# One causal attention and gated FFN layer on one core: one head's row moves on ScalarE's queue, new orders, the last row block in two column halves

## The reference

```
xn  = layernorm(x)                                   # no scale or shift
q   = xn @ w_q.T  (32 heads of 128), k, v = xn @ w_k.T, xn @ w_v.T (8 heads of 128)
p   = softmax(causal(q k^T / sqrt(128)))             # 4 query heads share a k/v head
s   = concat_heads(p @ v) @ w_dense.T
g   = silu(ffn(xn))    # three 512x512 layers of +1/-1 weights, two relu between
out = x + s * g
```

## Time and profile before

| | |
|---|---|
| median of 3 runs | 921.42 us (917.15 to 922.13) |
| the profiled execution | 921.1 us |
| its span, first to last instruction | 919.4 us |
| TensorE matmul busy | 895.9 us, 97% |
| VectorE, ScalarE, POOL busy | 650.1, 517.7, 480.9 us |
| mean granted TensorE clock | 0.996 of full speed |
| DMA queue of SyncE, share of the 16 DMA engines | 64.7% |

### The profile page before, as it was taken

One profiled execution on the slowest core, in us unless ns is written; L12 is line 12 of the kernel. 1 busy time (PEld: TensorE's weight loads), 2 busy tenths in 40 slices (PEclk: granted clock), 3 DMA queues, 4 the chain that ended last, 5 costly groups with the idle time before them and its releaser, 6 DMA issues.

```text
span 919.4 us, 15763 instructions
## 1 busy us (share of the span) xinstructions
PE 895.9 (97%) x4187; PEld 747.9 (81%) x4187; DVE 650.1 (71%) x1145; ACT 517.7 (56%) x1096; POOL 480.9 (52%) x388
## 2 busy tenths in 40 slices
PE   7999999999999999999999999989999999989997
PEld 6888888887878888888888887878878887778886
DVE  7436777777777787688767787767777786577844
ACT  4405665556546665466556654655556663475652
POOL 5302565546554665346654655445554754346674
PEclk9999999999999999999999999999999999999999
DMA  7176857577766866586747666684757675465662
GB/s 251 47 213 189 229 131 176 133 205 166 161 133 184 220 147 151 163 239 134 185 132 196 180 161 133 180 220 113 179 136 201 174 165 137 121 201 126 140 168 92
DMA packets 215561, 152.01 MB, mean 165 GB/s; under 512 B 23664, under 2 KB 180848, under 8 KB 215536
## 3 DMA queue, kind: packets, MB, share of 16 engines
q1 hardware_dynamic: 215536, 151.71, 64.7%
HBM read 67.90 MB, written 27.39 MB: 104 GB/s over the span
## 4 chain that ended last, share of the span: by engine, by line
issue 49%; POOL 31%; PE 15%; DMA 2%; DVE 1%; SPq 1%; POOLq 1%; ACT 0%; DVEq 0%
POOL pt_lo L830 22%; POOL w_lo L855 4%; POOL wd_lo L855 3%; PE ps_m L1341 3%; PE ps_m L1217 2%; PE ps_m L1219 2%; PE ps_m L1218 2%; PE ps_s L1326 2%; POOL v_lo L843 1%; PE ps_o L1217 1%; PE ps_o L1219 1%; PE ps_o L1218 1%; PE ps_s L1219 1%; PE ps_s L1218 1%; PE ps_s L1217 1%
## 5 line engine op out<-in xcount | busy, mean ns | idle before, releaser
L830 POOL TENSOR_TENSOR pt_lo<-pt_lo,pt_hi 128x512 fp32r<-128x512 f32 x248 | 324.1, 1334 | 308.8 <-ACT pt_hi L963 308.7
L1073 DVE CUSTOM_DVE_ANT_0 ps_s<-ps_s,mask 128x32 f32<-128x32 f32 (+31 forms) x256 | 181.5, 715 | 106.1 <-PE ps_s L1219 104.8
L963 ACT ACTIVATE pt_hi<-pt_lo 128x512 fp32r<-128x512 f32 x288 | 169.0, 627 | 102.2 <-PE ps_o L1219 58.4
L917 ACT ACTIVATE prob_odd<-ps_s,small 128x160 f32<-128x160 f32 (+15 forms) x128 | 95.9, 751 | 62.3 <-DVE small L1073 59.6
L1217 PE MATMUL ps_m<-xn_hi,w_hi 128*128 128x512 f32 x320 | 125.4, 392 | 2.2 <-DVE q_lo L1176 2.2
L1218 PE MATMUL ps_s<-k_lo,q_hi 128*128 128x480 f32 (+15 forms) x384 | 127.2, 331 | 0.0
L1219 PE MATMUL ps_s<-k_hi,q_lo 128*128 128x480 f32 (+15 forms) x384 | 126.8, 330 | 0.0
L1217 PE MATMUL ps_o<-pt_hi,v_hi 128*128 128x512 f32 x288 | 118.0, 410 | 8.4 <-POOL pt_lo L830 7.9
L1219 PE MATMUL ps_m<-xn_hi,w_lo 128*128 128x512 f32 x320 | 125.6, 393 | 0.0
L1218 PE MATMUL ps_m<-xn_lo,w_hi 128*128 128x512 f32 x320 | 125.4, 392 | 0.0
L1217 PE MATMUL ps_s<-k_hi,q_hi 128*128 128x480 f32 (+15 forms) x384 | 124.8, 325 | 0.0
(11 more groups left out here) (122 smaller groups left out, 1494.3 us busy)
## 6 DMA issues: line engine op xcount, KB each, us to landing
pt_lo<-prob_odd SPq DMA_DIRECT2D x128, 128.0 KB, 2.9
pt_lo<-prob_even SPq DMA_DIRECT2D x128, 112.0 KB, 2.3
pt_lo<-prob_odd SPq DMA_DIRECT2D x128, 96.0 KB, 2.2
raw<-wqk SPq DMA_DIRECT2D x40, 256.0 KB, 4.6
pt_lo<-prob_even SPq DMA_DIRECT2D x128, 80.0 KB, 2.6
inv_rows<-inv SPq DMA_DIRECT2D x32, 256.0 KB, 4.2
raw<-wd SPq DMA_DIRECT2D x32, 256.0 KB, 3.9
at_lo<-inv SPq DMA_DIRECT2D x32, 256.0 KB, 3.7
```

The lines of the kernel that those rows point to most:

```text
L830: pool.tensor_tensor(pt_lo[:, slot, :], pt_lo[:, slot, :].bitcast(F32), pt_hi[:, hi_slot, :], ALU.subtract).then_inc(land_lo, 1)
L917: act.activation(prob_tile(i, tile), as_tiles(score_row(i, tile)), ACT.Exp, scale=-1.0, bias=neg_max[:, slot:slot + 1], accum_out=row_sum[ ...
L963: act.activation(pt_hi[:, hi_slot, :], pt_lo[:, LAND_AT[i] + j, :].bitcast(F32), ACT.Copy).then_inc(land_hi, 1)
L1073: dve.tensor_tensor_reduce(out=scores, in0=scores, in1=mask[:, S - width(i % BLOCKS, tile):S], scale=-1.0, scalar=BIG, op0=ALU.add, op1=AL ...
```

## The change

Of each move of rows 4 to 7 the DMA of head 3 is issued by ScalarE, as a new token `amove.i.b` in its list; SyncE keeps heads 0 to 2. The lists of the body and of the last group are new on all engines, with the same tokens otherwise. In the last group dense.7 is done as two halves of 256 columns in the two banks, all 24 matmuls at the place of dense.7.3; its gate and its addition of x come before it (x + y * silu), and each half is multiplied by silu in place, added and stored by itself.

The diff; the POOL and VectorE lists of the body and most of the last group's lists are left out.

```diff
@@ -46,6 +46,8 @@
 BANKS4 = 4
 BY_DRAM = 4
 MOVES = TILES * HEADS
+
+ACT_HEADS = {i: (3,) for i in range(BY_DRAM, BLOCKS)}
 
 LANDS = [1 if n < BY_DRAM else MOVES for n in range(BLOCKS)]
 LANDINGS = (sum(LANDS[0::2]), sum(LANDS[1::2]))
...
 BODY = {
     "pe": """
-        unit.q2.1.0 scores.1.0 scores.1.1 scores.1.2 scores.1.3 unit.q2.1.1 unit.q2.1.2
-        unit.q2.1.3 scores.2.0 scores.2.1 unit.k.1.0 scores.2.2 scores.2.3 unit.k.1.1 weigh.0.0
-        scores.3.0 unit.k.1.2 scores.3.1 scores.3.2 unit.k.1.3 unit.q3.1.0 unit.q3.1.1 unit.q3.1.2
-        unit.q3.1.3 scores.3.3 unit.q0.1.0 unit.q0.1.1 unit.q0.1.2 unit.q0.1.3 unit.q1.1.0
-        unit.q1.1.1 unit.q1.1.2 unit.q1.1.3 dense.0.0 weigh.1.0 dense.0.1 weigh.1.1 scores.4.0
-        scores.4.1 dense.0.2 dense.0.3 unit.q1.0.0 scores.4.2 unit.q1.0.1 scores.4.3 unit.q1.0.2
-        scores.5.0 unit.q1.0.3 dense.1.0 dense.1.1 scores.5.1 scores.5.2 dense.1.2 weigh.2.0
-        dense.1.3 unit.q2.0.0 scores.5.3 weigh.2.1 scores.6.0 weigh.2.2 weigh.3.0 weigh.3.1
-        scores.6.1 weigh.3.2 unit.q2.0.1 unit.q2.0.2 weigh.3.3 unit.q2.0.3 dense.2.0 scores.6.2
-        dense.2.1 dense.2.2 dense.2.3 scores.6.3 unit.q0.0.0 unit.q0.0.1 scores.7.0 weigh.4.0
-        weigh.4.1 weigh.4.2 unit.q0.0.2 unit.q0.0.3 weigh.4.3 weigh.4.4 scores.7.1 scores.7.2
-        dense.3.0 weigh.5.0 dense.3.1 weigh.5.1 scores.7.3 dense.3.2 weigh.5.2 weigh.5.3 dense.3.3
-        weigh.5.4 weigh.5.5 unit.k.0.0 unit.k.0.1 unit.k.0.2 unit.k.0.3 unit.q3.0.0 unit.q3.0.1
-        weigh.6.6 unit.q3.0.2 unit.q3.0.3 dense.4.0 dense.4.1 dense.4.2 weigh.6.5 dense.4.3
-        scores.8.0 weigh.6.4 scores.8.1 weigh.6.3 weigh.6.2 scores.8.2 dense.5.0 scores.8.3
-        weigh.6.1 dense.5.1 dense.5.2 weigh.6.0 weigh.7.0 weigh.7.1 dense.5.3 weigh.7.2 weigh.7.3
-        weigh.7.4 weigh.7.5 weigh.7.6 weigh.7.7 dense.6.0 dense.6.1 dense.6.2 dense.6.3 dense.7.0
-        dense.7.1 dense.7.2 dense.7.3
+        scores.1.0 scores.1.1 scores.1.2 unit.q2.1.0 scores.1.3 unit.q2.1.1 scores.2.0 scores.2.1
+        unit.q2.1.2 scores.2.2 unit.q2.1.3 unit.q3.1.0 scores.2.3 unit.q3.1.1 unit.q3.1.2
+        scores.3.0 unit.q3.1.3 unit.q1.1.0 scores.3.1 scores.3.2 weigh.0.0 unit.q1.1.1 unit.q1.1.2
+        unit.q1.1.3 unit.k.1.0 unit.k.1.1 unit.k.1.2 scores.3.3 unit.k.1.3 unit.q0.1.0 unit.q0.1.1
+        unit.q0.1.2 unit.q0.1.3 dense.0.0 dense.0.1 dense.0.2 dense.0.3 scores.4.0 unit.q0.0.0
+        scores.4.1 unit.q0.0.1 scores.4.2 weigh.1.0 weigh.1.1 scores.4.3 unit.q0.0.2 scores.5.0
+        unit.q0.0.3 unit.q2.0.0 unit.q2.0.1 scores.5.1 unit.q2.0.2 scores.5.2 unit.q2.0.3
+        dense.1.0 dense.1.1 dense.1.2 scores.5.3 weigh.2.0 weigh.2.1 weigh.2.2 dense.1.3
+        scores.6.0 scores.6.1 weigh.3.0 weigh.3.1 weigh.3.2 weigh.3.3 dense.2.0 dense.2.1
+        dense.2.2 scores.6.2 scores.6.3 weigh.4.0 dense.2.3 unit.q1.0.0 unit.q1.0.1 weigh.4.1
+        unit.q1.0.2 scores.7.0 weigh.4.2 weigh.4.3 unit.q1.0.3 dense.3.0 scores.7.1 dense.3.1
+        weigh.4.4 scores.7.2 dense.3.2 weigh.5.0 scores.7.3 weigh.5.1 weigh.5.2 dense.3.3
+        weigh.5.3 unit.k.0.0 unit.k.0.1 weigh.5.4 weigh.5.5 unit.k.0.2 unit.k.0.3 unit.q3.0.0
+        unit.q3.0.1 unit.q3.0.2 unit.q3.0.3 dense.4.0 dense.4.1 dense.4.2 scores.8.0 dense.4.3
+        scores.8.1 scores.8.2 weigh.6.6 weigh.6.5 weigh.6.4 dense.5.0 weigh.6.3 weigh.6.2
+        dense.5.1 weigh.6.1 weigh.6.0 weigh.7.0 dense.5.2 weigh.7.1 dense.5.3 weigh.7.2 weigh.7.3
+        scores.8.3 weigh.7.4 weigh.7.5 weigh.7.6 weigh.7.7 dense.6.0 dense.6.1 dense.6.2 dense.6.3
+        dense.7.0 dense.7.1 dense.7.2 dense.7.3
     """,
     "act": """
-        exp.1.0 exp.1.1 exp.1.2 exp.1.3 hi.land.0.0 hi.unit.q2.1 hi.split.wd0 hi.split.wd1 exp.2.0
-        exp.2.1 exp.2.2 hi.split.wd2 exp.2.3 hi.weigh.0 hi.unit.k.1 exp.3.0 hi.split.wd3 exp.3.1
-        hi.unit.q3.1 exp.3.2 exp.3.3 hi.unit.q0.1 hi.land.1.0 hi.land.1.1 hi.split.q0 hi.unit.q1.1
-        hi.split.q1 hi.split.q2 hi.vload.1 hi.weigh.1 exp.4.0 exp.4.1 exp.4.2 exp.4.3 hi.unit.q1.0
-        exp.5.0 hi.land.2.0 hi.land.2.1 hi.land.2.2 exp.5.1 exp.5.2 hi.land.3.0 hi.land.3.1
-        hi.land.3.2 hi.split.q3 exp.5.3 hi.land.3.3 hi.split.k hi.weigh.2 exp.6.0 exp.6.1
-        hi.unit.q2.0 hi.land.4.0 hi.land.4.1 hi.land.4.2 hi.land.4.3 exp.6.2 hi.weigh.3 exp.6.3
-        hi.land.4.4 hi.unit.q0.0 exp.7.0 hi.land.5.0 hi.land.5.1 hi.land.5.2 hi.land.5.3 exp.7.1
-        hi.land.5.4 hi.land.5.5 hi.weigh.4 exp.7.2 exp.7.3 hi.land.6.6 hi.land.6.5 hi.unit.k.0
-        hi.land.6.4 hi.land.6.3 hi.land.6.2 hi.weigh.5 hi.unit.q3.0 hi.land.6.1 hi.land.6.0
-        exp.8.0 exp.8.1 exp.8.2 hi.land.7.0 hi.land.7.1 hi.land.7.2 exp.8.3 hi.land.7.3
-        hi.land.7.4 hi.land.7.5 hi.weigh.6 hi.land.7.6 hi.land.7.7 hi.weigh.7 hi.vload.0
+        exp.1.0 exp.1.1 exp.1.2 exp.1.3 exp.2.0 exp.2.1 hi.unit.q2.1 hi.land.0.0 exp.2.2
+        hi.split.wd0 exp.2.3 hi.unit.q3.1 hi.split.wd1 hi.split.wd2 hi.vload.1 exp.3.0 hi.weigh.0
+        hi.unit.q1.1 exp.3.1 hi.split.wd3 exp.3.2 hi.unit.k.1 exp.3.3 hi.unit.q0.1 hi.split.q0
+        hi.land.1.0 hi.land.1.1 hi.split.q1 exp.4.0 hi.split.q2 exp.4.1 exp.4.2 hi.weigh.1 exp.4.3
+        hi.unit.q0.0 exp.5.0 hi.land.2.0 hi.land.2.1 exp.5.1 hi.land.2.2 hi.unit.q2.0 exp.5.2
+        hi.land.3.0 amove.4.0 hi.land.3.1 hi.land.3.2 exp.5.3 hi.land.3.3 hi.weigh.2 amove.4.1
+        amove.4.2 amove.4.3 exp.6.0 exp.6.1 amove.5.0 hi.land.4.0 hi.land.4.1 hi.land.4.2
+        hi.land.4.3 exp.6.2 hi.weigh.3 exp.6.3 hi.land.4.4 amove.5.1 amove.5.2 amove.5.3
+        hi.split.q3 hi.split.k hi.unit.q1.0 exp.7.0 hi.land.5.0 hi.land.5.1 exp.7.1 hi.land.5.2
+        hi.land.5.3 hi.land.5.4 hi.weigh.4 exp.7.2 hi.land.5.5 exp.7.3 amove.6.0 amove.6.1
+        amove.6.2 amove.6.3 hi.unit.k.0 amove.7.0 amove.7.1 amove.7.2 hi.unit.q3.0 hi.land.6.6
+        hi.land.6.5 hi.land.6.4 hi.weigh.5 hi.land.6.3 amove.7.3 hi.land.6.2 hi.land.6.1
+        hi.land.6.0 exp.8.0 exp.8.1 hi.land.7.0 hi.land.7.1 hi.land.7.2 hi.land.7.3 exp.8.2
+        hi.land.7.4 hi.weigh.6 hi.land.7.5 hi.land.7.6 hi.land.7.7 exp.8.3 hi.weigh.7 hi.vload.0
     """,
...
     "sp": """
-        load.wd0 load.wd1 load.wd2 vload.1 dw.1 load.wd3 load.q0 rw.1 dr.1 load.q1 rr.1 load.q2
-        dw.2 rw.2 dw.3 load.q3 dr.2 rr.2 load.k rw.3 dr.3 move.4.0 move.4.1 move.4.2 move.4.3 rr.3
-        rw.4 move.5.0 move.5.1 move.5.2 move.5.3 rr.4 rw.5 move.6.0 move.6.1 move.6.2 move.6.3
-        rr.5 rw.6 move.7.0 move.7.1 move.7.2 move.7.3 rr.6 rw.7 rr.7 dw.8 vload.0 rw.8 dr.8 rr.8
+        load.wd0 load.wd1 load.wd2 vload.1 dw.1 rw.1 load.wd3 dw.2 load.q0 dr.1 load.q1 rr.1
+        load.q2 dr.2 rw.2 dw.3 load.q3 rw.3 load.k dr.3 rr.2 move.4.0 move.4.1 move.4.2 move.4.3
+        rr.3 rw.4 move.5.0 move.5.1 move.5.2 rr.4 move.5.3 rw.5 move.6.0 move.6.1 move.6.2
+        move.6.3 rr.5 rw.6 move.7.0 move.7.1 move.7.2 move.7.3 rr.6 rw.7 rr.7 vload.0 dw.8 rw.8
+        dr.8 rr.8
     """,
 }
 LAST = {
...
     "act": """
-        exp.1.0 exp.1.1 exp.1.2 exp.1.3 hi.land.0.0 exp.2.0 exp.2.1 hi.unit.q3.1 hi.split.wd0
-        exp.2.2 exp.2.3 hi.unit.q2.1 hi.split.wd1 hi.split.wd2 hi.vload.1 exp.3.0 hi.unit.q1.1
-        exp.3.1 hi.split.wd3 exp.3.2 hi.weigh.0 hi.unit.q0.1 hi.land.1.0 exp.3.3 hi.land.1.1
...
+        exp.1.0 exp.1.1 exp.1.2 exp.1.3 hi.land.0.0 exp.2.0 exp.2.1 hi.unit.q0.1 hi.split.wd0
+        exp.2.2 hi.split.wd1 hi.unit.q3.1 hi.split.wd2 exp.2.3 hi.vload.1 exp.3.0 hi.unit.q2.1
+        hi.weigh.0 hi.split.wd3 hi.unit.k.1 exp.3.1 hi.land.1.0 hi.unit.q1.1 build.0.0 build.0.1
+        build.0.2 build.0.3 exp.3.2 exp.3.3 hi.land.1.1 exp.4.0 build.1.0 build.1.1
...
     "dve": """
...
-        lo.hidden.1.1.3 gate.0 gate.1 lo.land.7.7 gate.2 mul.weigh.7 gate.3 lo.weigh.7 gate.4
-        lo.dense.6 gate.5 gate.6 lo.dense.7 gate.7 add_x.7
...
+        gate.5 lo.weigh.7 lo.dense.6 gate.6 gate.7 add_x.7
+        lo.dense.7
...
+HALVES = [slice(0, E // 2), slice(E // 2, E)]
 ROWS = [i[1] for i in ORDERS["last"]["dve"] if i[0] == "gate"]
 
 
@@ -582,6 +592,10 @@
 
             return ps_m[run.place(item) % 2] if item in run.order else None
 
+
+        def last_bank(run, part):
+
+            return ps_m[(run.place(("dense", BLOCKS - 1)) + part) % 2]
 
         x_loaded = [sem(f"x_loaded{b}") for b in range(BLOCKS)]
         scales_loaded = sem("scales_loaded")
@@ -637,6 +651,8 @@
         gated = sem("gated")
         scaled = sem("scaled")
         row_ready = sem("row_ready")
+        last_row_sum = sem("last_row_sum")
+        last_row_scaled = sem("last_row_scaled")
         last_row_ready = sem("last_row_ready")
 
         LN_STEPS = 6
@@ -757,7 +773,7 @@
                                 sp.sem_inc(flips_seen)
                                 sp.wait_ge(land_hi, r.pair(i - 2, COLUMNS[i - 2][0]))
                         slots = slice(LAND_AT[i], LAND_AT[i] + i + 1)
-                        for h in range(HEADS):
+                        for h in range(HEADS - len(ACT_HEADS.get(i, ()))):
```

(48 more changed lines are left out.)

164 lines of the change are left out of this document (83 added, 81 removed).

## The result

The changed kernel takes 930.86 us (median of 4 runs, 928.35 to 931.83), the kernel before 921.53 us beside it (4 runs): ratio 1.0103, 95% interval 1.007 to 1.0136. It is slower by 1%, about 9 us, where 910.0 was forecast, and lies outside the range of 902 to 921. The profiled execution has a span of 928.8 us and a mean granted clock of 0.986, against 919.4 and 0.996.

What follows compares the result with a forecast made beforehand. TensorE was taken to bound the kernel, waiting about 4.0 us a group for late landings. From 921.1 us, 9.1 for the bodies, 2.0 for the last group and 0 for the halves gave 910.0; own range 904 to 916, 80% range 902 to 921.

Steps and rivals of the forecast that it cites:

- part 2: New body orders: more TensorE work between most rows' last score tile and first weigh; period 99.6 against 100.9 us.
- Row 7: 0.9 us less lead, 1.8 us sooner landing: 0.9 better: Body, row 7: less TensorE work before its first weigh, sooner landing; half of a stall up to 1 us goes.
- the 0.8 us "for waits that the new orders bring": Body: allowance added to the best period of 98.8 us, giving 99.6 us a group.
- Part 1: Moves of rows 4 to 7: SyncE's 12 take 7.9 us, 2.6 less; ScalarE's four cost 0.6 us each.
- Row 7 gains 1.8 us: Row 7's landing: 9.0 us of DMA work in 10.8 us, so it can come 1.8 us sooner, not 2.6.
- Row 6 no gain: Row 6's landing: ScalarE's four moves stand behind exp.7.3, when SyncE's 12 are out; costed at no gain.
- row 4, named as the one that may be late next: Body, row 4: 3.3 us less lead, up to 2.6 given back by issue.
- the term of 9.1 us: Seven bodies: 1.3 us a group gained, 7 x 1.3 = 9.1 us; bounds 28 gained, and nothing or a loss.
- Part 3: Last group: load.k0 and the v load leave some 2 us sooner; 2.0 us gained, bounds 0 and 5.
- Part 4: Last row in halves, behind the last matmul: worth 0, between −0.5 and +1 us.
- rival B: ScalarE's in-order queue becomes the holder: at 0.9 us an issue, 3.0 us a group lost, 931 us; chance 0.12.
- A: Transfers don't come sooner, body stalls only move, only the last group's 2.0 us come: 919.1; chance 0.22, shared with another rival.

Runs made afterwards that it cites:

- the mended one: Changed kernel with weigh.4.4, flip.6.3, weigh.5.4 and weigh.5.5 sooner, and dr.1, rr.1 ahead of load.k2 in the last group: 904.0 us; without any split 911.89 us.
- the run of the split alone: Kernel before with only head 3's moves of rows 4 to 7 issued by ScalarE, in the seven bodies: 915.9 us, ratio 0.9949.
- row 6's gate mended: Changed kernel with weigh.4.4 right behind weigh.4.3 on TensorE and flip.6.3 ahead of lo.unit.q1.0 on VectorE: 910.88 us, ratio 0.9872.
- the run with the last group mended: Changed kernel with dr.1 and rr.1 ahead of load.k2 in SyncE's list of the last group: 923.62 us, ratio 1.0033.

## Why the prediction was wrong

**The step that failed** is in part 2, the row "Row 7: 0.9 us less lead, 1.8 us sooner landing: 0.9 better". Both numbers were wrong. The lead was counted from the row's last score tile, and that is not where the wait begins: SyncE's rows of the kernel before already showed that rows 6 and 7 leave one behind the other, and that weigh.4.4 starts them. From there the lead shrank by 3.7 us, and the first hi copy came sooner by 0.7 to 2.1 over the seven bodies. The 1.8 us took the DMA engines' busy share for the time that a row needs; row 7 took as long as before. The rule in `LAND_AFTER` and the place of the weigh tokens in both lists would have given the lead. In the sum the failed step is the 0.8 us "for waits that the new orders bring": waits before weigh.7.0 and the stretches behind them came to 3.4 us a body, so that a body took 714.6 / 7 = 102.1 us instead of 99.6. Moving the one token back gave 18 us (912.52), moving it away in the old orders cost 29 (948.43).

**Part 1.** The issue costs were right: mostly 0.60 us on ScalarE, 0.80 each in row 7's first three of the fourth body, 0.87 at most, and TensorE waited for exps only 0.5 us in all. Its effects stood at the wrong rows. "Row 7 gains 1.8 us" was at most half a microsecond of landing (904.8 against 904.0 us with and without); the window had 0.83 x 10.8 = 9.0 us of DMA work, but the row took 12.5 us from first issue to first hi copy with 12 issues as with 16. "Row 6 no gain" held for its landing in the changed kernel (12.4 to 13.6 us, 12.3 before), while in the old orders, where ScalarE's four moves go out spread over the burst and not bunched at its end, it was 0.8 to 1.3 us. What the part left out is what SyncE does with the time: it comes to row 7 1.0 to 1.7 us sooner behind weigh.4.4. Rows 4 and 5 landed later behind their first issues than before (12.7 to 14.1 us instead of 12.0, and 12.3 to 13.6 instead of 12.1 to 13.1). The split as a whole was worth 4 us in the old orders, 9 in the changed kernel and 8 in the mended one. The Trainium skill ("DMA: Bandwidth & Descriptors", section "Issuing engines are not separate DMA queues") says that a second issuer saves only issue time, usually small beside the transfer. The runs agree with the first half: row 7, where the transfers last, gained next to nothing, and what was saved is SyncE's time, 10.6 to 8.2 us for row 6. Here that was not small, as the run of the split alone shows.

**Part 2, the other rows.** Row 3's wait is gone from the bodies, and row 4, named as the one that may be late next, costs at most 0.34 us a body before weigh.4.0. With row 6's gate mended the bodies take 99.3 us each, 99.6 was forecast: the term of 9.1 us was near for these orders but for the one token, though row 7's line in it stood on a wrong reason.

**Part 3.** 2.0 us were forecast; the group became 1.3 us longer. The v load did go out 2.6 us sooner after the group's start and its wait fell by 2.2 us, but a second wait of 2.13 us for row 1's writes took part of that back, and the move of load.k2 ahead of dr.1 was not priced at all. It cost 3.95 us from start to start, less one matmul (3.78 as idle time), and the stretch at 1.2 GHz behind it; without it the group is 4.4 us shorter than before, inside the bounds of 0 to 5.

**Part 4.** Forecast 0, measured 0.1 less; in the one profile of the halves alone the end was 1.5 us shorter, and the new order of the end took that away. Dense.6 and two gates were counted, the POOL addition beside add_x.7 (0.9 us more) was not.

**The rivals.** The time landed on rival B's 931, but not by B: its point, 0.9 us an issue, was not reached, and without the `amove` tokens the kernel is slower still (939.79); that the number fits is chance. A's words, that the body's stalls only move, describe the body best; it gave no price to the new place. That rows 6 and 7 form one chain stood in no rival.

**Open.** Of the 23.3 us of the fourth body from weigh.4.4 to row 7's first hi copy the first 10.8 are SyncE's own issuing; how much of the other 12.5 comes from row 6's transfers, which still run then, was not separated. The 1.1 us before the first body are taken as chance because the code is the same; no kernel has two profiles that would show it.

## What to carry to other kernels

Count a transfer's lead from the event that lets it start: the release of its buffer, and the end of what stands ahead of it in the same queue. Where two bursts follow each other in one queue, the first one's gate is the second one's too, and while the queue is still at the first, an earlier gate of the second brings nothing. A load that waits for a ring slot belongs behind every DMA in its queue that someone is waiting for.

## What was not expected of the hardware

- Issues got slower while the other queue was moving blocks of the same row: SyncE's 12 of row 7 took 8.82 us, 0.73 each (single ones up to 1.39 over the bodies), where 16 alone take 10.61, 0.66 each, in the kernel before and in the run with row 7's split taken out. From row 7's first issue to its last landing the mean was 12.9 us in both kernels.
- One addition of 128x512 on VectorE took 1.59 us while POOL did one of its own, against 0.69 where POOL did nothing. POOL's took 1.60 us beside it, against 1.29 in the run with the halves alone.
- A wait of 3.18 us cost TensorE 2.7 us more in the 1.2 GHz stretch behind it. The length of the wait alone does not tell whether one follows: waits of 2.12 and 2.18 us had one, while four of 2.7 to 3.3 us in the run with all moves on SyncE and two (2.74 and 2.92) in the run with the last group mended had none. So 11.5 us less waiting before weigh.7.0 (15.9 to 4.4) came with 20 us less time.
